# Edge stage of a graph transformer layer: the one-hot's transposes and the target scores in one product

## The reference

```python
# graph attention, 4 heads of 64; each node also has an edge to itself
h = (xn @ W).reshape(n, 4, 64)
a_src, a_dst = sum(h * att_src, -1), sum(h * att_dst, -1)
e = leaky_relu(a_src[src] + a_dst[dst], 0.2)
ex = exp(e - segment_max(e, dst)[dst])
alpha = ex / (segment_sum(ex, dst)[dst] + 1e-16)
gat = segment_sum(h[src] * alpha, dst) + bias      # then + xn, layer norm, relu
# linear attention, 8 heads: q, k = elu(.) + 1
kv = einsum(k, v); z = 1 / (q . sum(k) + 1e-6)
mix = einsum(q, kv, z) @ w_out + b_out             # then + xn, rms norm
x = x + gat + mix
x = x + experts(layernorm(x))                      # top 2 of 8, gelu
```

## Time and profile before

| | |
|---|---|
| median of 3 runs | 3567.93 us (3563.46 to 3569.03) |
| profiled execution, span | 4403.2 us |
| PE busy | 3041.5 us (69%) |
| PE weight loads busy | 2470.3 us (56%) |
| DVE busy | 2365.2 us (54%) |
| POOL busy | 2160.0 us (49%) |
| ACT busy | 1275.7 us (29%) |

### The profile page before, as it was taken

How to read it: one execution, slowest core, us unless ns; L and a number is a source line. 1 busy time by engine, 2 the same in 40 slices (tenths; PEclk the granted TensorE clock), 3 DMA queues, 4 the chain that set the end, 5 groups by cost and what they waited for, 6 DMA issues and landing times. The chain is left out here.

```text
span 4403.2 us, 70224 instructions
## 1 busy us (share of the span) xinstructions
PE 3041.5 (69%) x17326; PEld 2470.3 (56%) x17327; DVE 2365.2 (54%) x6486; ACT 1275.7 (29%) x4257; POOL 2160.0 (49%) x2117
## 2 busy tenths in 40 slices
PE   6566666666676776666666777676323349999998
PEld 5444545545555554455555555555323349999997
DVE  7544444444444444545555555555788865555554
ACT  6422222222222222222222222222455523333332
POOL 3255555555555555444444544444066644444444
PEclk9778777878888887878888888888555559999999
DMA  7544444444444444444444444444455724444443
GB/s 262 173 117 117 111 115 112 119 108 111 109 119 111 115 114 117 121 126 121 128 126 122 133 126 125 126 120 111 127 169 186 238 96 71 72 70 72 70 71 55
DMA packets 384652, 529.69 MB, mean 120 GB/s; under 512 B 64276, under 2 KB 323559, under 8 KB 384218
## 3 DMA queue, kind: packets, MB, share of 16 engines
q0 software_dynamic: 114496, 265.49, 25.5%
q1 hardware_dynamic: 185112, 183.84, 14.8%
q10 hardware_dynamic: 84770, 77.19, 5.5%
HBM read 394.80 MB, written 132.72 MB: 120 GB/s over the span
## 5 line engine op out<-in xcount | busy, mean ns | idle before, releaser
L1133 POOL DMA_INDIRECT rows<-node_rows,index x1552 | 1480.9, 954 | 1392.6 <-SPq L1102 930.3
L1411 PE MATMUL ps_sum<-msg,hot 128*128 128x260 f32 x3904 | 1220.7, 465 | 40.0 <-issue 27.9
L1411 PEld LDWEIGHTS ps_sum<-msg,hot 128*128 128x128 f32 x3904 | 853.5, 230 | 198.4 <-issue 45.3
L1391 PE MATMUL ps_hot<-ident_h,hotT 128*128 128x128 bf16 x1952 | 223.5, 247 | 729.7 <-ACT hot L1293 338.6
L1391 PEld LDWEIGHTS ps_hot<-ident_h,hotT 128*128 128x128 bf16 x1952 | 154.3, 110 | 832.8 <-issue 549.4
L1213 DVE TENSOR_TENSOR msg<-rows,ps_w 128x1024 f32<-128x1024 f32 x488 | 596.1, 1222 | 45.1 <-ACT ps_w L1305 29.1
L2140 POOL DMA_INDIRECT out_dram<-big x204 | 352.7, 1729 | 438.3 <-DVE big L2232 390.9
L1195 DVE TENSOR_REDUCE e<-ps_tgt 128x32 f32<-128x96 f32 x488 | 123.3, 253 | 801.2 <-remote 728.2
L1293 ACT ACTIVATE hot<-ps_hot 128x512 f32<-128x512 bf16 x488 | 290.2, 595 | 736.3 <-remote 589.0
L2166 PEld LDWEIGHTS x_ps_hT<-x_rowsT,x_w_now 128*128 128x128 f32 x3264 | 398.0, 192 | 11.5 <-DVE x_w_now L2210 1.1
L2166 PE MATMUL x_ps_hT<-x_rowsT,x_w_now 128*128 128x128 f32 x3264 | 399.1, 276 | 0.7 <-DVE x_w_now L2210 0.7
(11 more groups left out here) (289 smaller groups left out, 4194.9 us busy)
## 6 DMA issues: line engine op xcount, KB each, us to landing
targets<-dst_row SPq DMA_DIRECT2D x391, 128.0 KB
big<-expert_in SPq DMA_DIRECT2D x204, 130.0 KB
rows<-node_rows,index POOLq DMA_INDIRECT x1564
node_rows<-big SPq DMA_DIRECT2D x14, 924.0 KB
turned<-rT SPq DMA_DIRECT2D x14, 896.0 KB, 4.6
area<-turned ACTq DMA_DIRECT2D x98, 128.0 KB
queries<-area ACTq DMA_DIRECT2D x98, 128.0 KB
area<-queries ACTq DMA_DIRECT2D x98, 128.0 KB
```

What stands on the lines that cost most here:

```text
L1133: g.indirect_dma_start(rows[:, j, k, :], None, s.node_rows, bass.IndirectOffsetOnAxis(ap=index[:, b, j * G + k:j * G + k + 1], axis=0)).th ...
L1391: mm = pe.transpose(ps_hot[:, k * P:(k + 1) * P], hotT[:, j % 2, k * P:(k + 1) * P], ident_h[:, :])
L1411: mm = pe.matmul(ps_sum[:, j % 2, 0:SUM], hot[:, j % MSGS, k * P:(k + 1) * P], msg[:, j % MSGS, k, :], start=(k == 0), stop=(k == G - 1))
```

## The change

The transposes and the target scores of a pair become one product for each group of 128 edges. Its moving operand, `turn_and_reach`, holds the identity (128 columns, written once) and beside it the 24 score columns of the pair's window, which DVE copies in for every pair ahead of the one-hot; there are two such buffers. The result, ps_edge, is float32 with 256 numbers to a group, in the two banks that ps_hot and ps_tgt had; there is one of it. `fold` reads its last 24 columns of each group, and `copy_hot` the first 128. `copy_hot` now waits for `fold` of its pair. PE's product waits for the new copy, the one-hot, and `copy_hot` of the pair before. The lags are as they were, and PE no longer loads the window numbers.

```diff
+WIDE_REACH = PARTS * 2 * GH
...
-        ident_h = sb("ident_h", [P, P], BF16)
+        turn_and_reach = sb("turn_and_reach", [P, 2, P + WIDE_REACH], BF16)
...
-        ps_hot = ctx.enter_context(nc.psum_tensor("ps_hot", [P, 1024], BF16))
-        ps_tgt = ctx.enter_context(nc.psum_tensor("ps_tgt", [P, 512], F32))
+        ps_edge = ctx.enter_context(nc.psum_tensor("ps_edge", [P, G, 256], F32))
...
             @block.vector
-                v.tensor_copy(ident_h[:, :], s.ident[:, :]).then_inc(table_ready, 1)
+                for u in range(2):
+                    v.tensor_copy(turn_and_reach[:, u, 0:P], s.ident[:, :]).then_inc(table_ready, 1)
...
                 def one_hot(n, j):
...
-                    from_item(v, tgt_psum, n, 2, n - 1)
+                    from_item(v, edge_psum, n, 2, n - 1)
+                    w = v.snap(windows[j], min_val=0, max_val=WINDOWS - 1)
+                    v.tensor_copy(turn_and_reach[:, j % 2, P:P + WIDE_REACH],
+                                  reach_parts[:, bass.ds(w, 1), :, :].rearrange("p t q k -> p (t q k)")).then_inc(reach_set, 1)
                     v.tensor_scalar(hotT[:, j % 2, :], targets[:, bass.ds(here, 1), :].rearrange("p j n -> p (j n)"),
                                     plan.node_id[:, n:n + 1], None, ALU.is_equal).then_inc(hotT_ready, 1)
 
                 def fold(n, j):
-                    v.wait_ge(tgt_psum, n + 1)
+                    v.wait_ge(edge_psum, n + 1)
                     v.tensor_reduce(e1[:, j % 2, :, :],
-                                    ps_tgt[:, 0:G * PARTS * 2 * GH].rearrange("p (g q k) -> p g k q", g=G, q=PARTS),
+                                    ps_edge[:, :, P:P + WIDE_REACH].rearrange("p g (q k) -> p g k q", q=PARTS),
                                     AX.X, ALU.add).then_inc(tgt_folded, 1)
...
             @block.scalar
                 def copy_hot(n, j):
-                    act.wait_ge(turned, n + 1)
+                    act.wait_ge(tgt_folded, n + 1)
                     from_item(act, sum_psum, n, MSGS, n - (MSGS - 1))
-                    act.activation(hot[:, j % MSGS, :], ps_hot[:, 0:SPAN], ACT.Copy).then_inc(hot_ready, 1)
+                    act.activation(hot[:, j % MSGS, :].rearrange("p (g n) -> p g n", g=G), ps_edge[:, :, 0:P], ACT.Copy).then_inc(hot_ready, 1)
...
             @block.tensor
-                def turn_hot(n, j):
+                def turn_and_look_up(n, j):
                     pe.wait_ge(hotT_ready, n + 1)
+                    pe.wait_ge(reach_set, n + 1)
                     from_item(pe, hot_ready, n, 1, n)
                     for k in range(G):
-                        mm = pe.transpose(ps_hot[:, k * P:(k + 1) * P], hotT[:, j % 2, k * P:(k + 1) * P], ident_h[:, :])
-                    mm.then_inc(turned, 1)
-
-                def target_scores(n, j):
-                    if j % 4 == 0:
-                        pe.load(windows, plan.window[n // PAIR_RING:n // PAIR_RING + 1, j:j + 4])
-                    w = pe.snap(windows[j % 4], min_val=0, max_val=WINDOWS - 1)
-                    from_item(pe, tgt_folded, n, 1, n)
-                    wide = PARTS * 2 * GH
-                    for k in range(G):
-                        mm = pe.matmul(ps_tgt[:, k * wide:(k + 1) * wide], hotT[:, j % 2, k * P:(k + 1) * P],
-                                       reach_parts[:, bass.ds(w, 1), :, :].rearrange("p t q k -> p (t q k)"), start=True, stop=True)
-                    mm.then_inc(tgt_psum, 1)
+                        mm = pe.matmul(ps_edge[:, k, 0:P + WIDE_REACH], hotT[:, j % 2, k * P:(k + 1) * P], turn_and_reach[:, j % 2, :],
+                                       start=True, stop=True)
+                    mm.then_inc(edge_psum, 1)
...
-                in_pairs([turn_hot, target_scores, sum_pair], [0, 0, 3],
+                in_pairs([turn_and_look_up, sum_pair], [0, 3],
```

More of the change, by code:

```diff
@@ L1016, in attend_edges @@
         hotT_ready = sem("c_hotT_ready")
-        turned = sem("c_turned")
+        reach_set = sem("c_reach_set")
         hot_ready = sem("c_hot_ready")
-        tgt_psum = sem("c_tgt_psum")
+        edge_psum = sem("c_edge_psum")
         tgt_folded = sem("c_tgt_folded")
@@ L1153, in _ @@
                     if q + 1 < PARTS:
-                        v.wait_ge(table_ready, q + 2)
+                        v.wait_ge(table_ready, q + 3)
                         v.tensor_tensor(reach[:, :, :], reach[:, :, :], reach_parts[:, :, q, :], ALU.subtract).then_inc(table_step, 1)
@@ L1370, in _ @@
                 act.wait_ge(blank_set, 2)
-                act.wait_ge(table_ready, 1 + PARTS)
+                act.wait_ge(table_ready, 2 + PARTS)
                 act.dma_start(out[N:N + P, :], blank[:, 0, 0:D]).then_inc(blank_stored, 16)
@@ L1383, in _ @@
             def _(pe):
-                pe.wait_ge(table_ready, 1 + PARTS)
-                windows = [pe.alloc_register(f"pe_window{k}") for k in range(4)]
-                def turn_hot(n, j):
+                pe.wait_ge(table_ready, 2 + PARTS)
+                def turn_and_look_up(n, j):
                     pe.wait_ge(hotT_ready, n + 1)
+                    pe.wait_ge(reach_set, n + 1)
                     from_item(pe, hot_ready, n, 1, n)
                     for k in range(G):
-                        mm = pe.transpose(ps_hot[:, k * P:(k + 1) * P], hotT[:, j % 2, k * P:(k + 1) * P], ident_h[:, :])
-                    mm.then_inc(turned, 1)
-                def target_scores(n, j):
-                    if j % 4 == 0:
-                        pe.load(windows, plan.window[n // PAIR_RING:n // PAIR_RING + 1, j:j + 4])
-                    w = pe.snap(windows[j % 4], min_val=0, max_val=WINDOWS - 1)
-                    from_item(pe, tgt_folded, n, 1, n)
-                    wide = PARTS * 2 * GH
-                    for k in range(G):
-                        mm = pe.matmul(ps_tgt[:, k * wide:(k + 1) * wide], hotT[:, j % 2, k * P:(k + 1) * P],
-                                       reach_parts[:, bass.ds(w, 1), :, :].rearrange("p t q k -> p (t q k)"), start=True, stop=True)
-                    mm.then_inc(tgt_psum, 1)
+                        mm = pe.matmul(ps_edge[:, k, 0:P + WIDE_REACH], hotT[:, j % 2, k * P:(k + 1) * P], turn_and_reach[:, j % 2, :],
+                                       start=True, stop=True)
+                    mm.then_inc(edge_psum, 1)
                 def sum_pair(n, j):
```

## The result

The changed kernel takes 3692.94 us (median of 4 runs, 3688.55 to 3695.7) against 3568.48 (4 runs, 3563.46 to 3569.64): ratio 1.0354, 95% interval 1.0336 to 1.0373, 124 us slower. The prediction said 3675 (3580 to 3770), slower.

A forecast was written before the change was run, and what follows sets the result against it. In the edge stage, part A (key and value tiles) was bound by POOL's gathers, part B (mixing tiles) by add_xn and project_out taking turns. Waits and copy 132 us, less 25 for PE's clock, 107 on 3568: 3675 us (3580 to 3770).

The forecast's parts named there:

- The moved wait: Edge stage: ACT's copy_hot waits for fold, PE's next product for copy_hot; with VectorE's copy 132 us more at full clock.
- The ring: DVE and PE taking turns in an add_xn iteration of the mixing part: 6.23 us after the change instead of 5.38.
- The term for an add_xn pair: Mixing part, iteration in which DVE's add_xn waits for project_out: 0.85 us more.
- The stall of weigh: DVE's weigh waits for ACT's exponentials, now behind the later one-hot copy: taken 0.30 us per pair.
- the new turn of a plain pair: Mixing part, pair without add_xn: 0.47 us more, from weigh's stall and VectorE's copy.
- The term for the clock: Mixing part: PE at 1.2 GHz for a quarter of it lags in both kernels, hiding the later copy: 25 us less.
- The combined iteration's price: Mixing tiles three pairs apart, divide and add_xn in one iteration: between 0.2 and 0.85 us more, taken 0.35.
- the third rival: Worse lock-step: ACT's mixing steps ahead of a copy, 1 us per tile, or PE longer at 1.2 GHz; 3773 us, chance 0.17.
- VectorE's copy: DVE's copy of 24 bf16 score columns ahead of each one-hot: 0.10 to 0.30 us, taken 0.17, on the mixing part's path.
- The first rival (hidden): The mixing part already goes at its gathers' 841 us, or fold waits for PE: 3568 to 3600 us, chances 0.06 and 0.05.
- the second (PE paces B): Faster: PE paces the mixing part, only its shorter work counts; 30 to 46 us less, about 3530 us, chance 0.09.
- the fourth (gathers held up): VectorE's new copies delay POOL's gathers in the key and value part: 42 us on top, 3717 us, chance 0.05.

The follow-up runs named there:

- the earlier trace: First profile of the kernel before, unchanged: span 4403.2 us, with late releases in the edge stage; its timed runs had a median of 3567.9 us.
- the run with filler: Changed kernel plus twenty dummy 128-column products on PE behind each of the 98 project_out: 3653.32 us, ratio 1.024.
- the one with the moved wait: Kernel before with only copy_hot waiting for fold instead of the turns: 3722.39 us; with twenty dummy products behind each project_out 3664.82 us.

## Why the prediction was right, and where its terms were off

*What bounds the stage: right.* A at its gathers, B at the turns of add_xn and project_out, some 100 us above its own gathers (941 against 840). The late add_xn shows it: the same work, with add_xn and measure one pair later, waits for no project_out, and B falls from 941 to 834 us, where 841 was given as the floor.

*The moved wait: right, and more than the whole loss.* The ring was predicted as 1.40 + 0.45 + 3.58 + 0.80 = 6.23 us and is 1.42 + 0.26 + 3.56 + 0.82 = 6.06. The order of fold, copy and product is the cause: turned round, or shortened by an earlier fold, the same work costs 16 or 26 us.

*The term for an add_xn pair was too large*: 0.85 us taken, 0.57 in the mean measured with PE at its higher level (6.09 against 5.52; 0.67 by the middle values). Most of the difference is the step from the product to the sum, 0.26 instead of 0.45: the sum's first row follows the four products' start by about the 0.25 us that I had named as the lower bound (4 x 152 columns at 2.4 GHz), not near the 0.58 of the two old groups. The row to go by was the bound, since one group without register steps behind it is unlike the old pair of groups. The stall of weigh (0.30 taken, 0.31 in the rows) and the new turn of a plain pair (0.47 taken, 0.41 measured) were close. With the table's means at the higher level the waits give 68 x 0.40 + 64 x 0.32 + 65 x 0.57 + 33 x 0.34 = 96 us in B; the prediction had 127 there.

*The term for the clock had the wrong sign.* I read the 0.82 of the earlier trace rows as a state of PE that both kernels would share, in which PE lags and hides the later copy, and took off 25 us. That 0.82 belonged to the execution with the late releases: without them it is 0.97. And the lower level comes from the change itself. The changed kernel, around one pair with divide and add_xn, first in the timeline, then by the busy time of three stretches:

```profile
1997.04 0.42 PE L1395 MATMUL ps_edge<-turn_and_reach,hotT 128*128 128x152 bf16 x4 [2.56 <-ACT hot L1297]
...
1997.30 3.05 PE L1405 MATMUL ps_sum<-msg,hot 128*128 128x260 f32 x8
...
2001.45 0.43 PE L1395 MATMUL ps_edge<-turn_and_reach,hotT 128*128 128x152 bf16 x4
```

```profile
1994.00:1997.20 3.20, 0.64 (x6) 0.26 (x5) 2.36 (x8) 0.78 (x3) 2.59 (x3) 1.00 0.51 144
1997.30:2000.35 3.05, 3.05 (x12) 2.35 (x10) 2.71 (x8) 1.22 (x5) 1.89 (x2) 0.62 0.61 156
2001.50:2003.80 2.30, 2.18 (x13) 1.59 (x11) 1.99 (x9) 0.66 (x3) 1.74 (x2) 1.00 0.92 303
```

PE worked 0.64 of the 3.20 us before 1997.2, waiting for add_xn, fold and copy; the sum behind it then ran mostly at 1.2 GHz (3.05 us instead of 1.97), and the next product came at 2001.45, behind the mixing products and with no wait of its own: PE had become the late one. Of the 33 pairs with divide and add_xn 17 met the lower level, in the mean 7.32 us against 6.39 for the other 16. Five of these 16 start within 0.4 us of the end of a stretch at 1.2 GHz and take 7.12 us each; the other 11 take 6.06 in the mean, close to the 6.05 of the run with filler. One of the five begins on DVE at 2254.38; PE comes late into it, out of a sum of 3.63 us. That sum, then the busy time of the stretch at 1.2 GHz and of the pair:

```profile
2250.67 3.63 PE L1405 MATMUL ps_sum<-msg,hot 128*128 128x260 f32 x8
```

```profile
2250.65:2254.00 3.35, 3.35 (x11) 2.67 (x9) 3.01 (x8) 0.99 (x4) 0.94 (x1) 0.50 0.55 157
2254.40:2261.50 7.10, 6.18 (x37) 4.74 (x34) 4.07 (x14) 1.67 (x6) 4.73 (x5) 1.00 0.59 154
```

So 22 of the 33 pairs are long beside the lower level, not 17, and the dummy products gave back more than the 17 alone had led me to expect. The combined iteration's price of 0.35 us was right for PE at its higher level (0.34), and 1.01 in the run. The Trainium skill, TensorE: Matmul & The Clock Gate, "A second HAM failure mode: psum-queue depth-cycling", describes a kernel whose PE idles briefly between groups of products and so swings between its two levels, and pays at each swing; 46 stretches against 13, and none once the idle time is filled, agree with it.

So 132 - 25 = 107 came out near the 124 by luck, because two terms erred against each other: 33 too much (132 against 96 and 3 of the tail) and 47 too little (-25 against +22), with A where it was. The forecast's own range was also added up loosely: its terms, -46 and +72, give 3629 to 3747, and it said 3620 to 3740. The second half of the third rival ("a PE that idles longer and is at 1.2 GHz for more of B") was the part of it that happened; ACT's mixing steps, its first half, were not seen ahead of the copy by 1 us per tile: at the higher level B is below the forecast.

*VectorE's copy.* 0.17 us taken for it on the path. Its start stands 0.13 us ahead of the one-hot's in the median (0.07 to 0.13 in most pairs); alone it costs 12 us, 0.05 per pair of B in the mean.

*The first rival (hidden), the second (PE paces B) and the fourth (gathers held up) did not happen.* A did not grow with 248 new copies on VectorE, and the middle gather is 946 ns in both (949 in the earlier trace rows):

```profile
L1133 POOL DMA_INDIRECT rows<-node_rows,index x1552: 940/946/1191, 205.9 to 2369.5; - x194
```

By the rule of the Trainium skill, SBUF — State Buffer, "Who interferes with whom", each of these copies could have held POOL up; neither the length of A nor the middle gather of this trace shows any of it.

*Not settled.* Whether ACT and DVE could read ps_edge at the same time, with no order between copy and fold, wasn't tried: both would touch the same banks at once. Why the first profiled execution of the kernel before had its late releases is open too.

## What to carry to other kernels

When one result replaces two, count what the single buffer makes wait: here the fused product, VectorE's copy included, saved 11 us, and the order that it imposed, copy after fold with the next product still behind the copy, cost 114. Price such a wait where two engines already go in turns, and look first for the step that makes them do so: moving add_xn one pair later was worth 97 us, more than the change could have brought, and made the change free. And the wait that added idle time to PE between groups of products was paid a second time here, in its clock (157 us of B at 1.2 GHz against 48): such a term goes in with a plus.

## What was not expected of the hardware

The kernel was faster with more work on PE: 98 x 20 dummy products, 1.28 us per mixing tile, took 40 us off the changed kernel, 58 off the one with the moved wait and 16 off the kernel before. In B of the changed kernel the granted clock fell to 1.2 GHz 46 times, the fall shown above in the sum that followed 3.20 us in which PE had worked 0.64.

A profiled execution can differ from the runs by much more than the runs from each other: 4403.2 us with late releases in the edge stage, 3565.0 the next time. Terms of a sum that rest on its stretches (the clock of 0.82 above all) did not carry over; distances between rows that no such wait touched did.
